# One of every 24 row gathers of a graph-attention kernel becomes a one-hot product on TensorE

## The chip, the cores and the metric

The kernel runs on one NeuronCore of one Trainium2 chip. The metric is the device time of one execution in microseconds (us). The core has five engines that run their own instruction streams and wait for one another through semaphores: TensorE (PE in the profile), VectorE (DVE), ScalarE (ACT), GpSimd (POOL) and SyncE (SP), which here issues most DMAs.

## The reference, cut to what matters

A graph of 6,250 nodes with 64 features and 206,250 edges, sorted by destination, goes through one mean-aggregating layer and three attention layers. Each attention layer is this (heads H = 2, 2, 1; C = 64 / H):

```python
q = (x @ Wq + bq).reshape(n, H, C)
k = (x @ Wk + bk).reshape(n, H, C)
v = (x @ Wv + bv).reshape(n, H, C)
e = (eattr @ We).reshape(-1, H, C)
kj = k[src] + e
alpha = jnp.sum(q[dst] * kj, axis=-1) / jnp.sqrt(C)
m = segment_max(alpha, dst); a = jnp.exp(alpha - m[dst])
a = a / (segment_sum(a, dst)[dst] + 1e-16)
vj = v[src] + e
out = segment_sum(a[..., None] * vj, dst)       # then + x @ Ws + bs
```

What the change is about is `k[src]` and `v[src]`: for each edge, 64 + 64 numbers of the row of its source node.

## The kernel before

The edges are cut into 202 blocks of 1,024. A block is T = 8 tiles of 128 edges, one edge per partition. Each attention layer first runs a node phase, which computes for all nodes a table `KV` of 128 float32 per node (k and v side by side) and a table `QT`, and stores both to DRAM. Then an edge pass goes over the blocks. For each block:

- POOL fetches the rows of the source nodes: `gathers` issues 8 indirect DMAs, one for each tile (L1621), into the tile buffer `G` (named `Gall` in the profile), of which there are three, one for each of three successive blocks. The row numbers come from `sdn`. The first gather of a block waits until PE has done step `aT` of the block three earlier.
- PE computes the edge part `e` (L896, L901: 512 columns, float32), picks the queries with a one-hot product (`q`, L921), transposes alpha (`aT`, L928), transposes the scan's result back (`Fb`, L933), carries maxima through one-hot products (`Mc` L936, `Mn` L948, `Me` L955) and sums the weighted values of a block (`fac` L966, `agg` L963).
- DVE adds and multiplies (`kj` L754, `vj` L759, `prod` L765, `alpha` L770), makes the one-hot tables (`OT` L733, `O` L722), does a running maximum (`scan` L784) and small work on the maxima (`fhi`, `fm`, `flo` L787 and L800, `cr` L807, `X` to `df` L811 to L825), weights the values (`vals` L842) and adds them to `acc` (L869, L890).
- ACT does the exponentials and some copies. SP issues the other loads.

The order of work is written by hand: `vector_step`, `tensor_step` and `scalar_step` each hold one step `t`, in which an engine works on five blocks at different stages (Z for block t+2, A for t+1, B for t, C for t-1, D for t-2). Three steps make one turn of the hardware loop, because the buffers have three slots. Each engine has one counting semaphore, and `after(e, engine, op, s)` waits until that engine has passed operation `op` of block `s`. A layer ends in a drain (`vector_drain`, `tensor_drain`) with its own order for the last blocks.

So in each step, PE's order is Fb, q, fac and agg, Mc, Mn, e, aT, Me, and the next step's Fb.

The mean layer's edge pass is simpler (PE: 512 columns `e`, `agg`, `q`), and has no gathers.

Of the kernel before, what the change touches and what calls it, by code (L numbers as in the profile page):

```python
# [16 lines left out]
T = 8  # L17
BE = 128 * T
BIAS = 6
W = 42  # L20
SL = 4


class Sizes:
    def __init__(self, n, e):
        self.n = n
        self.e = e
        self.blocks = -(-e // BE)
# [38 lines left out]
def build(nc, z, a, ctx):  # L67
    B, NCOL, NT, SM = z.blocks, z.nc, z.tiles, z.smax
    N = z.n

# [11 lines left out]
    WK = sb("WK", [128, NT, 64])  # L82
    hT = sb("hT", [65, NCOL])
# [14 lines left out]
    ioi = sb("ioi", [128, SM], I32)  # L98
    iof = sb("iof", [128, SM])
# [18 lines left out]
    rq = sb("rq", [128, SL, 4, 64])
# [4 lines left out]
    dnarrow = Gall[:, B * T:B * T + B * T // 2].bitcast(I16)  # L123
    sdn = [sb(f"sdn{u}", [128, 3 * T], I32) for u in range(3)]
# [39 lines left out]
    pIo = pM[:, 6 * T:6 * T + W]  # L164
    pFac = pG[0:66, 64:65]
    pFacS = pS[0:66, 200:201]

# [4 lines left out]
    D16 = dram("D16", [B, BE], I16)  # L172
    KV = [dram(f"KV{l}", [NCOL, 128]) for l in range(3)]
# [6 lines left out]
    def row(v, m):  # L180
# [7 lines left out]
    s_o = sem("out_landed")  # L188
    su_V, su_P, su_G, su_A = sem("setup_V"), sem("setup_P"), sem("setup_G"), sem("setup_A")
# [6 lines left out]
                 "cb", "cbh0", "cbh1", "rowf", "rowf4", "row1", "row2", "row12", "rowin", "thirds", "below", "third", "rowbase", "narrow", "iop"] + [f"qz{u}" for u in range(3)]  # L196
# [47 lines left out]
    def vector_setup(e):  # L244
# [92 lines left out]
        e.tensor_copy(pIo, iof[:, 0:W]).then_inc(su_V, 1)  # L337
        for u in range(3):
            e.memset(qw[u][:, :], 0.0).then_inc(su_V, 1)
# [20 lines left out]

    NG = -(-NT // 4)
# [7 lines left out]
    def node_phase(name, kind, w, H, kv, qt):  # L369
# [8 lines left out]
        before_kv, before_qt = {}, {}  # L378
        for c in range(NG if tables else 0):
            before_qt[c] = qt_landed[c % SL]  # L380
            qt_landed[c % SL] += 16
            if kv is not None:
                before_kv[c] = kv_landed[c % SL]
                kv_landed[c % SL] += 16
# [153 lines left out]
        def rows_A(e, c):  # L538
            g, m = c % SL, tiles_of[c]
            if before_kv[c]:  # L540
                e.wait_ge(s_kv[g], before_kv[c])
            e.wait_ge(own["P"], pP["mm", c])
            e.activation(stg[:, g, 0:m, 0:128], kv_bank[c % 2][:, 0:128 * m].rearrange("p (t c) -> p t c", t=m),
                         ACT.Copy).then_inc(own["A"], 1)

        def query_A(e, c):
            g, m = c % SL, tiles_of[c]
            both = q_bank[c % 2][:, 0:128 * m].rearrange("p (t c) -> p t c", t=m)
            if c >= SL:
                e.wait_ge(own["V"], pV["lo", c - SL])  # L550
            e.wait_ge(own["P"], pP["qs", c])
            e.activation(stg[:, g, 0:m, 128:192], both[:, :, 0:64], ACT.Copy).then_inc(own["A"], 1)
# [4 lines left out]
            e.activation(stq[:, g, 0:m, 0:64], stg[:, g, 0:m, 128:192], ACT.Copy).then_inc(own["A"], 1)  # L557

        def sync(e):
            if kv is not None:  # L560
                for c in range(NG):
                    e.wait_ge(own["A"], pA["ev", c])
                    e.dma_start(kv[512 * c:512 * c + 128 * tiles_of[c], :].rearrange("(t p) c -> p t c", p=128),
                                stg[:, c % SL, 0:tiles_of[c], 0:128]).then_inc(s_kv[c % SL], 16)
# [72 lines left out]
        def query_V(e, c):  # L637
            g, m4 = c % SL, tiles_of[c]
            hi, lo, mi = (stq[:, g, 0:m4, 64 * k:64 * k + 64] for k in range(3))
            rr = rq[:, g, 0:m4, :]  # L640
            e.wait_ge(own["A"], pA["hi", c])
            e.tensor_tensor(rr, stg[:, g, 0:m4, 128:192], hi, ALU.subtract).then_inc(own["V"], 1)
# [13 lines left out]
    def edge_pass(name, kind, l, heads, qtab, kvtab, eat):  # L656
# [9 lines left out]
        if att:  # L666
            order = {
                "V": ["A kj", "A vj", "B fhi", "B fm", "B flo", "B cr", "Z OT", "A prod", "A alpha", "C d1", "C d",
                      "Z cont", "Z last", "A flag", "A O", "B X", "B Mhi", "B Mm", "B Mlo", "B df", "C vals",
                      "D facc", "D acc", "A scan"],  # L670
                "P": ["B Fb", "A q", "D agg7", "B Mn", "Z e", "A aT", "B Me"],
                "A": ["A tb", "C w", "C wide", "A lb", "A Ob", "B fb", "B fbw"],
            }
        else:
            order = {
                "V": ["C acc", "Z O", "Z OT"],
                "P": ["A e", "B agg7", "A q"],
                "A": ["A relu"],
            }
# [13 lines left out]
        sums = [pG, pG, pG] if att else [pG, pQ, pY]  # L693
        columns = pIo if att else iof[:, 0:W]
# [16 lines left out]

        def ge16(e, sems, per, s):
            e.wait_ge(sems[s.slot], s.times(16 * per, 16 * per))


        def v_O(e, s):
# [3 lines left out]
            else:  # L720
                ge16(e, s_i, 1, s)
# [25 lines left out]

        def v_kj(e, s):
            u = s.slot
            ge16(e, s_g, T, s)  # L750
# [114 lines left out]
        def v_facc(e, s, fac=pFac, preset=False):  # L865
            if not preset:
                base_of[s.c] = base_at(e, s)
            c = acc[0:AR, bass.ds(base_of[s.c], 1)]
# [95 lines left out]

        def p_fac(e, s, fac=pFac):
# [39 lines left out]
        nV = place(["fhi1", "fm1", "flo1", "cr1", "d1_2", "d_2", "flag0", "vals2", "facc3", "acc3",  # L1005
# [7 lines left out]
        def vector_drain(e, n):  # L1013
# [4 lines left out]
            after(e, "V", "scan", s1)  # L1018
            e.wait_ge(dP, nP["Fb1"])
# [23 lines left out]
            ge16(e, s_g, T, s0)  # L1043
# [60 lines left out]
        def one_hot(e, s):  # L1104
# [4 lines left out]
                iof[:, 0:W].unsqueeze(1).to_broadcast([128, T, W]), ALU.subtract, ALU.is_equal)  # L1109
# [20 lines left out]
        def tensor_drain(e, n):  # L1130
# [7 lines left out]
            p_q(e, s0, T - 1).then_inc(dP, 1)  # L1138
            p_fac(e, s3)
            for j in range(T - 1):  # L1140
                p_agg(e, s3, j)
            p_agg(e, s3, T - 1).then_inc(dP, 1)
# [12 lines left out]
            for j in range(T - 1):  # L1155
                p_agg(e, s2, j)
            p_agg(e, s2, T - 1).then_inc(dP, 1)
# [10 lines left out]
            p_agg(e, s1, 0)  # L1168
# [5 lines left out]
            for j in range(1, 4):  # L1174
                p_agg(e, s1, j)
# [3 lines left out]
            for j in range(4, T - 1):  # L1179
                p_agg(e, s1, j)  # L1180
            p_agg(e, s1, T - 1).then_inc(dP, 1)
# [61 lines left out]

        def vector_step(e, t, on):
            pV = prog["V"]
            zt, at, bt, ct, dt = t + 2, t + 1, t, t - 1, t - 2
            if not att:
# [4 lines left out]
                if "Z" in on:  # L1252
                    v_O(e, zt).then_inc(pV, 1)
                    v_OT(e, zt).then_inc(pV, 1)
                else:
                    missing(e, "V", t, "O", "OT")
                return
            if "A" in on:
                v_kj(e, at).then_inc(pV, 1)
                v_vj(e, at).then_inc(pV, 1)  # L1260
            else:
                missing(e, "V", t, "kj", "vj")
# [31 lines left out]
            else:  # L1294
                missing(e, "V", t, "flag", "O")
            if "B" in on:
# [13 lines left out]
            if "D" in on:  # L1310
# [4 lines left out]
                v_facc(e, dt).then_inc(pV, 1)  # L1315
# [8 lines left out]
        def tensor_step(e, t, on):  # L1324
# [30 lines left out]
            if "D" in on:  # L1355
                after(e, "V", "acc", dt - 1)
                hold(e)
                p_fac(e, dt)
# [19 lines left out]
            else:  # L1378
                missing(e, "P", t, "aT", "aT")
            if "B" in on:  # L1380
# [152 lines left out]

        def load_rows(e, s, b, base):
# [33 lines left out]
        def sync_step(e, s):  # L1568
# [7 lines left out]
            load_rows(e, s, b, base)  # L1576

        def sync(e, ready):
# [3 lines left out]
            for c in range(3):  # L1582
                load_rows(e, At(0, c), *first_places[c])
            for c in range(3, 3 + z.peel):
                sync_step(e, At(0, c))
            with e.Fori(0, n) as i:
                for c in range(3 + z.peel, 6 + z.peel):
                    sync_step(e, At(i, c))

# [18 lines left out]
        def gathers(e, s):  # L1608
# [3 lines left out]
            for j in range(T):  # L1612
# [45 lines left out]
    def _(e):  # L1658
# [4 lines left out]
        for l in range(3):  # L1663
            att_pass[l]["E"](e, [(fold_V, l + 1), (s_dn, 16)])
            before[l]["S"](e)
            att_pass[l]["S"](e, before[l]["q_tables"])
# [30 lines left out]
    def _(e):  # L1697
# [6 lines left out]
        mean_end["V"](e, [(fold_V, 1)])  # L1704
        for l in range(3):
# [6 lines left out]
    def _(e):  # L1712
# [3 lines left out]
        mean_end["P"](e, [(fold_V, 1)])  # L1716
        for l in range(3):
            att_pass[l]["P"](e, [(Mb_V, l + 1), before[l]["done"]["A"], before[l]["done"]["V"]])
# [59 lines left out]
```

## Time and profile before

| | us |
|---|---|
| median of 3 runs | 6819.26 (6818.12 to 6822.41) |
| the profiled execution | 6818.34 |
| its span in the trace | 6816.5 |
| busy in the span: PE | 4422.8 (65%) |
| DVE | 4366.3 (64%) |
| ACT | 1118.9 (16%) |
| POOL | 4726.5 (69%) |

The span is what the trace covers; the profiled execution's own time is 1.8 us longer. The mean layer's edge pass runs from about 80 to 527 us, and the three attention passes with their node phases fill the rest. A busy share is an average over the engine; what an engine waits for, and for how long, has to be read from the waits.

### The profile page before, as it was taken

Reading aid. Unit: us, or ns where it says so; the run is one execution under the profiler, and the core shown is the slowest. Engines: PE = TensorE matmul, PEld = TensorE weight load, DVE = VectorE, ACT = ScalarE, POOL = GpSimd, SP = SyncE. Lnnn points to the kernel's source line nnn. Section 1 sums busy time; section 2 is a strip of 40 time slices with the busy share of each in tenths; the row PEclk is TensorE's granted clock in tenths of the full one; section 3 lists DMA queues with packets and bytes.
Section 4 is the critical chain, followed back from the end, with each engine's and each line's share of the span. In section 5 each row is a group of like instructions: output and inputs, shape, how many; then the busy total and the mean of one; then the engine's idle time right before and its main releaser. Section 6 shows DMA issues by size and latency. Waiting matters only on the chain. (4 is left out here: it accounts for less than half of the span.)

```text
span 6816.5 us, 149747 instructions
## 1 busy us (share of the span) xinstructions
PE 4422.8 (65%) x36620; PEld 3475.0 (51%) x36620; DVE 4366.3 (64%) x15732; ACT 1118.9 (16%) x4722; POOL 4726.5 (69%) x5116
## 2 busy tenths in 40 slices
PE   7996666666666667666666666667666666666665
PEld 5775444444444446444444444446444444444444
DVE  5556666666666666666666666666666666666666
ACT  3222111111111112111111111112111111111111
POOL 1224777777777775777777777775777777777776
PEclk9995555555555555555555555555555555555555
DMA  4553333333333333333333333333333333333333
GB/s 128 159 159 96 95 95 95 96 95 95 95 96 95 96 95 98 95 95 95 95 95 95 95 95 95 95 96 97 95 95 95 95 95 96 95 95 95 96 96 80
DMA packets 687682, 675.79 MB, mean 99 GB/s; under 512 B 369234, under 2 KB 506388, under 8 KB 687636
## 3 DMA queue, kind: packets, MB, share of 16 engines
q0 software_dynamic: 161600, 320.52, 18.3%
q1 hardware_dynamic: 496944, 301.76, 16.3%
q10 hardware_dynamic: 29092, 52.97, 2.6%
q8 instruction: 19, 0.31, 0.0%
q14 instruction: 27, 0.22, 0.0%
HBM read 652.96 MB, written 21.67 MB: 99 GB/s over the span
## 5 line engine op out<-in xcount | busy, mean ns | idle before, releaser
L1621 POOL DMA_INDIRECT Gall<-KV,sdn x4848 | 4590.0, 947 | 1517.0 <-issue 1380.9
L754 DVE TENSOR_TENSOR kj<-Gall,pE 128x512 f32<-128x512 f32 x603 | 414.4, 687 | 1973.4 <-DMA Gall<-KV,sdn 1971.3
L963 PE MATMUL pG<-O,vals 128*66 128x42 f32 (+1 forms) x10736 | 1291.9, 308 | 0.7 <-ACTq L1242 0.7
L963 PEld LDWEIGHTS pG<-O,vals 128*66 128x66 f32 (+1 forms) x10736 | 1200.8, 223 | 47.4 <-ACT vals L1002 28.4
L948 PE MATMUL pY<-fw,Ob 128*42 128x6 bf16 (+1 forms) x4800 | 255.1, 176 | 1139.9 <-DVE cr L807 1139.9
L994 ACT ACTIVATE vals<-dd 128x16 f32<-128x16 f32 (+1 forms) x606 | 131.6, 217 | 4679.5 <-DVE dd L834 4671.0
L948 PEld LDWEIGHTS pY<-fw,Ob 128*42 128x42 bf16 x4800 | 220.4, 121 | 1192.9 <-issue 1192.9
L896 PE MATMUL pE<-bd,ea 128*128 128x256 f32 x1212 | 739.9, 714 | 13.6 <-PEq L1242 13.6
L955 PEld LDWEIGHTS pM<-Mb,OTs 42*128 42x128 bf16 x4800 | 176.3, 101 | 921.1 <-issue 921.1
L901 PE MATMUL pE<-bd,ea 128*128 128x256 f32 x1212 | 642.8, 634 | 0.0
L955 PE MATMUL pM<-Mb,OTs 42*128 42x6 bf16 (+1 forms) x4800 | 209.9, 163 | 514.2 <-DVE df L825 511.8
L933 PE MATMUL pS<-ident,Fs 16*128 16x16 f32 (+1 forms) x600 | 150.0, 250 | 598.9 <-DVE Fs L784 567.9
L901 PEld LDWEIGHTS pE<-bd,ea 128*128 128x128 f32 x1212 | 408.7, 337 | 108.5
L933 PEld LDWEIGHTS pS<-ident,Fs 16*128 16x128 f32 (+1 forms) x600 | 105.9, 177 | 633.2 <-issue 633.2
L770 DVE TENSOR_REDUCE al<-kj 128x16 f32<-128x512 f32 (+1 forms) x603 | 414.3, 687 | 20.8
L733 DVE TENSOR_SCALAR OTs<-db,bfp 128x1024 bf16<-128x1024 int16 x808 | 408.0, 505 | 20.6 <-DMA dr<-in_dr 17.8
L759 DVE TENSOR_TENSOR vj<-Gall,pE 128x512 f32<-128x512 f32 x606 | 412.3, 680 | 0.0
L765 DVE TENSOR_TENSOR kj<-kj,pQ 128x512 f32<-128x512 f32 x603 | 408.4, 677 | 0.0
L842 DVE TENSOR_TENSOR vals<-vj,pE 128x512 f32<-128x512 f32 x597 | 401.4, 672 | 0.0
L1518 POOL DMA_DIRECT2D sdn<-in_sdn x202 | 108.8, 539 | 406.0 <-DVE OTs L733 334.5
L921 PE MATMUL pQ<-qw,OTs 128*128 128x64 bf16 x4848 | 367.5, 241 | 7.9 <-DVE OTs L733 5.2
L722 DVE SCALAR_TENSOR_TENSOR O<-sdn,bf,pM 128x336 f32<-128x336 int32 x603 | 329.1, 546 | 0.0
(223 smaller groups left out, 6539.9 us busy)
## 6 DMA issues: line engine op xcount, KB each, us to landing
db<-D SPq DMA_DIRECT2D x606, 256.0 KB
ea<-in_ea SPq DMA_DIRECT2D x606, 128.0 KB
Gall<-KV,sdn POOLq DMA_INDIRECT x4848
db<-D ACTq DMA_DIRECT2D x202, 256.0 KB, 3.5
qw<-QT SPq DMA_DIRECT2D x1818, 5.2 KB
dr<-in_dr SPq DMA_DIRECT2D x1212, 4.0 KB
ea<-in_ea SPq DMA_DIRECT2D x202, 64.0 KB, 3.3
sdn<-in_sdn SPq DMA_DIRECT2D x606, 12.0 KB
```

Source lines behind the costliest of these rows:

```text
L733: return e.tensor_scalar(OTs[u][:, :, :].rearrange("p j m -> p (j m)"), db[u][:, :], bfp[:, bass.ds(s.value(), 1)], None, ALU.is_equal)
L754: return e.tensor_tensor(kj[:, :, :], G[u][:, :, 0:64], pE[u][:, :].rearrange("p (j c) -> p j c", c=64), ALU.add)
L759: return e.tensor_tensor(vj[u][:, :, :], G[u][:, :, 64:128], pE[u][:, :].rearrange("p (j c) -> p j c", c=64), ALU.add)
L765: return e.tensor_tensor(kj[:, :, :], kj[:, :, :], pQ[:, :].rearrange("p (j c) -> p j c", c=64), ALU.mult)
L770: return e.tensor_reduce(al[u][:, 0:H * T].rearrange("p (h j) -> p j h", h=H), kj[:, :, :].rearrange("p j (h c) -> p j h c", h=H), AX.X, A ...
L842: return e.tensor_tensor(vals[u][:, :, 0:64].rearrange("p j (h c) -> p j h c", h=H), vj[u][:, :, :].rearrange("p j (h c) -> p j h c", h=H) ...
L896: return e.matmul(pE[u][:, 0:256], ea[u][:, 0:128], bd32[:, l, :], start=True, stop=True)
L901: return e.matmul(pE[u][:, 256:512], ea[u][:, 128:256], bd32[:, l, :], start=True, stop=True)
L948: return e.matmul(pmn[:, j, :], lhs, rhs, start=False, stop=j == T)
L955: return e.matmul(pme[:, j, :], OTs[u][0:W, j, :], Mb[:, 0:3 * H], start=True, stop=True)
L963: return e.matmul(out[0:AR, 0:W], vals[u][:, j, 0:AR], O[u][:, j, :], start=j == 0, stop=j == T - 1)
L1621: e.indirect_dma_start(G[u][:, j, :], None, kvtab, bass.IndirectOffsetOnAxis(ap=sdn[u][:, j:j + 1], axis=0)).then_inc(s_g[u], 16)
```

## The change

The table `KV` of a layer, 50 tiles of 128 nodes, is now also kept in SBUF (`KVS`). For every third block (`picks`), POOL issues 7 gathers and not 8. The eighth tile's rows come from TensorE: PE multiplies a one-hot table `oh` (128 nodes by 128 edges) with four tiles of `KVS` at a time (128x512, float32) and accumulates over all 50 tiles in the bank `pG`. That leaves, for each edge and each of four candidates (the node number's quarter), one row of 128 numbers, and DVE picks the right one with six small operations (`v_sel`) and writes it to the eighth tile of `G`. The 13 matmuls of such a pick are spread over three steps (4, 4 and 5, one of them with 256 columns), each share as `gp` between `aT` and `Me`. DVE makes the one-hot tables (`v_oh`, one in each step, behind `O`), from a row of keys `kb` that SP loads once in three steps from a small table `K16`. That table is made once, behind the mean layer, from source numbers which DVE collects in the mean pass (`v_src`).

Beside that: `agg` and `fac` write to the bank `pY` where they wrote to `pG`, `v_facc` waits for `aT` too, the node phase evicts k and v straight into `KVS` (no wait for a staging slot), and some small tables of the setup lie in `KVS` for the time of the setup.

```diff
+        def v_sel(e, s, inc, n):
+            u = s.slot
+            to = G[u][:, LAST, :]
+            e.tensor_scalar(quarter[:, :], sdn[u][:, LAST:T], 7, 3, ALU.logical_shift_right,
+                            ALU.bitwise_and).then_inc(sel_V, 1)
+            e.wait_ge(sel_V, sel_at(s, 0))
+            e.tensor_tensor(msk[:, :], ioq[:, :], quarter[:, :].to_broadcast([128, 4]),
+                            ALU.is_equal).then_inc(sel_V, 1)
+            e.wait_ge(sel_V, sel_at(s, 1))
+            after(e, "P", "gp", s - 1)
+            e.tensor_scalar(to, pPick[:, 0, :], msk[:, 0:1], None, ALU.mult).then_inc(sel_V, 1)
+            for k in range(1, 4):
+                e.wait_ge(sel_V, sel_at(s, k + 1))
+                i = e.scalar_tensor_tensor(to, pPick[:, k, :], msk[:, k:k + 1], to, ALU.mult, ALU.add)
...
+        def v_oh(e, s):
+            k = (s.slot - pick_slot) % 3
+            m, f = PIECE[k], FROM[k]
+            if k == 0:
+                e.wait_ge(s_k, s.times(16, 16 * (2 - first_pick // 3)))
+            return e.scalar_tensor_tensor(
+                oh[s.slot][:, 0:m, :], kb[:, :].unsqueeze(1).to_broadcast([128, m, 128]), prow[:, 0:1],
+                pQd[:, f:f + m].unsqueeze(2).to_broadcast([128, m, 128]), ALU.subtract, ALU.is_equal)
...
+        def p_gp(e, s):
+            k = (s.slot - pick_slot) % 3
+            after(e, "V", "oh", s)
+            hold(e)
+            if k == 0 and picks(s):
+                after(e, "V", "sel", s)
+                hold(e)
+            for n in range(PIECE[k]):
+                q = order_q[FROM[k] + n]
+                m = min(4, NT - 4 * q)
+                p = e.matmul(pG[:, 0:128 * m], oh[s.slot][:, n, :],
+                             KVS[:, 4 * q:4 * q + m, :].rearrange("p t c -> p (t c)"),
+                             start=k == 0 and n == 0, stop=k == 2 and n == PIECE[k] - 1)
+            return p
...
             if "A" in on:
-                v_kj(e, at).then_inc(pV, 1)
+                if picks(at):
+                    v_sel(e, at, pV, 1)
+                v_kj(e, at).then_inc(pV, 1 if picks(at) else 2)
                 v_vj(e, at).then_inc(pV, 1)
...
+            if made(zt):
+                v_oh(e, zt).then_inc(pV, 1)
...
+            if made(at):
+                p_gp(e, at).then_inc(pP, 1)
...
-            for j in range(T):
+            for j in range(T - 1 if picks(s) else T):
```

On TensorE, in the loop of the first attention pass, one step stood like this before (from `e` of block t+2 to the next step's `agg`; `ident,al` is `aT`, `Mb,OTs` is `Me`, `ident,Fs` is `Fb`):

```order
L896 MATMUL pE<-bd,ea 128x256
L901 MATMUL pE<-bd,ea 128x256
L702 REGISTER_ALU
L928 MATMUL pS<-ident,al 16x128
L702 REGISTER_ALU
L955 MATMUL pM<-Mb,OTs 128x6 x8
L702 REGISTER_ALU
L933 MATMUL pS<-ident,Fs 128x16
L921 MATMUL pQ<-qw,OTs 128x64 x8
L702 REGISTER_ALU
L966 MATMUL pG<-e,fb 66x1
L963 MATMUL pG<-O,vals 66x42 x8
```

After the change the same place reads:

```order
L1014 MATMUL pE<-bd,ea 128x256
L766 REGISTER_ALU
L1041 MATMUL pS<-ident,al 16x128
L766 REGISTER_ALU x2
L1088 MATMUL pG<-KVS,oh 128x512 x4
L766 REGISTER_ALU
L1068 MATMUL pM<-Mb,OTs 128x6 x8
L766 REGISTER_ALU
L1046 MATMUL pS<-ident,Fs 128x16
L1034 MATMUL pQ<-qw,OTs 128x64 x8
```

The share `gp` (L1088) now stands behind `aT` and ahead of `Me`, of the next step's `Fb` and of all that follows.

On VectorE, at the start of the loop's turn in which the block is a picked one, this stands ahead of `kj` (L866) and `vj` (L871):

```order
L834 TENSOR_SCALAR quarter<-sdn 128x1
L836 ISA
L837 TENSOR_TENSOR msk<-ioq,quarter 128x4
L839 REGISTER_ALU
L766 ISA
L841 TENSOR_SCALAR Gall<-pG,msk 128x128
L843 REGISTER_ALU
L844 SCALAR_TENSOR_TENSOR Gall<-pG,msk,Gall 128x128
```

Two more of the last row follow, then `kj`; `kj` was the first operation of the step before.

On GpSimd, the loop's body of the first attention pass (three blocks) was this before:

```order
L1630 ISA
L702 ISA
L1621 DMA Gall<-KV,sdn 128x128 x8
L702 REGISTER_ALU
L1621 DMA Gall<-KV,sdn 128x128 x8
L713 REGISTER_ALU
L702 REGISTER_ALU
L1621 DMA Gall<-KV,sdn 128x128 x8
```

And after the change:

```order
L1791 ISA
L766 ISA
L1782 DMA Gall<-KV,sdn 128x128 x8
L766 REGISTER_ALU
L1782 DMA Gall<-KV,sdn 128x128 x8
L791 REGISTER_ALU
L766 REGISTER_ALU
L1782 DMA Gall<-KV,sdn 128x128 x7
```

One gather of the three blocks' 24 is gone. Ahead of the loop 77 gathers stand where 80 stood; with 64 turns of the loop that makes 3 + 64 = 67 fewer in a layer, 201 in all.

## Rows read from the trace of the kernel before

**Rows 1.** The page: granted TensorE clock in 40 slices, and the group of gathers.

```profile
PEclk9995555555555555555555555555555555555555
...
L1621 POOL DMA_INDIRECT Gall<-KV,sdn x4848 | 4590.0, 947 | 1517.0 <-issue 1380.9
```

**Rows 2.** The waits between 3400 and 4400 us: us in total, times, longest.

```profile
DVE kj L754 <- DMA Gall<-KV,sdn: 328.1, 100, 4.1
POOL Gall L1621 <- issue: 229.8, 754, 0.3
...
PE pY L948 <- DVE cr L807: 185.2, 100, 2.7
```

**Rows 3.** The timeline of PE over one step: start, us, engine, line.

```profile
3500.21 1.22 PE L896 MATMUL pE<-bd,ea 128*128 128x256 f32 x2
...
3502.07 0.42 PE L928 MATMUL pS<-ident,al 128*16 128x128 f32 x1
3503.40 0.35 PE L955 MATMUL pM<-Mb,OTs 42*128 42x6 bf16 x8 [0.91 <-DVE df L825]
3504.75 0.26 PE L933 MATMUL pS<-ident,Fs 16*128 16x16 f32 x1 [1.00 <-DVE Fs L784]
3504.94 0.61 PE L921 MATMUL pQ<-qw,OTs 128*128 128x64 bf16 x8
...
3507.75 0.23 PE L936 MATMUL pY<-cb,onb 1*42 1x54 bf16 x1
3509.45 0.42 PE L948 MATMUL pY<-fw,Ob 128*42 128x6 bf16 x8 [1.46 <-DVE cr L807]
...
3509.84 1.22 PE L896 MATMUL pE<-bd,ea 128*128 128x256 f32 x2
```

**Rows 4.** Groups by form between 3400 and 4400 us: busy, mean ns.

```profile
L754 DVE TENSOR_TENSOR kj<-Gall,pE 128x512 f32<-128x512 f32 x100 | 68.8, 688 | 328.1 <-DMA Gall<-KV,sdn 328.1
...
L776 DVE TENSOR_TENSOR flg<-tb 16x127 f32<-16x127 f32 x100 | 28.4, 284 | 0.0
```

**Rows 5.** The timeline of PE in the mean layer's edge pass.

```profile
303.62 1.09 PE L963 MATMUL pY<-O,vals 128*65 128x42 f32 x16
304.53 0.41 PE L921 MATMUL pE<-qw,OTs 128*128 128x64 bf16 x8
304.77 1.10 PE L897 MATMUL pE<-bd,ea 128*128 128x512 f32 x2
305.72 0.50 PE L963 MATMUL pG<-O,vals 128*65 128x42 f32 x6
```

**Rows 6.** PE in stretches: length, busy (instructions), granted clock, DMA share, GB/s.

```profile
528.00:530.00 2.00, 0.82 (x14) 1.00 0.00 0
530.00:532.00 2.00, 1.06 (x10) 0.61 0.00 0
...
548.00:550.00 2.00, 2.00 (x11) 0.50 0.00 0
550.00:552.00 2.00, 2.00 (x16) 0.77 0.00 0
552.00:554.00 2.00, 0.75 (x7) 1.00 0.00 0
554.00:556.00 2.00, 0.00 (x0) 0.58 0.00 0
592.00:594.00 2.00, 2.00 (x11) 0.50 0.58 147
3400.00:4400.00 1000.00, 625.71 (x5000) 0.50 0.36 95
```

**Rows 7.** The timeline of PE where the dense stretch at 547 us begins.

```profile
547.17 1.06 PE L478 MATMUL pE<-ident,WK 128*64 128x128 f32 x4
```

**Rows 8.** The timeline of PE inside the stretch at 592 us.

```profile
592.83 1.92 PE L499 MATMUL pQ<-wn,hT 65*128 65x128 f32 x8
```

**Rows 9.** The timeline of POOL at the first attention layer's end.

```profile
2614.29 0.94 POOL L1621 DMA_INDIRECT Gall<-KV,sdn  x1 [0.31 <-issue]
```

**Rows 10.** The timeline of DVE there.

```profile
2613.25 0.40 DVE L784 TENSOR_TENSOR_SCAN Fs<-flg,pS 16x128 f32<-16x128 f32 x1
2615.37 0.17 DVE L787 TENSOR_TENSOR fw<-pS,lm 128x16 bf16<-128x16 f32 x1 [1.72 <-PE pQ L921]
...
2619.68 0.69 DVE L1044 TENSOR_TENSOR kj<-Gall,pE 128x512 f32<-128x512 f32 x1 [0.59 <-DMA Gall<-KV,sdn]
```

**Rows 11.** All engines in the same long stretch: PE, PEld, DVE, ACT, POOL busy, clock.

```profile
3400.00:4400.00 1000.00, 625.71 (x5000) 491.75 (x4998) 650.86 (x2396) 145.42 (x700) 756.49 (x800) 0.50 0.36 95
```

More of the change, by code:

```diff
@@ L21 @@
 SL = 4
+LAST = T - 1
 class Sizes:
@@ L123, in build @@
     dnarrow = Gall[:, B * T:B * T + B * T // 2].bitcast(I16)
+    srcT = sb("srcT", [128, 4 * KG])
+    kb = sb("kb", [128, 128], I16)
+    oh = [sb(f"oh{u}", [128, PIECE[2], 128]) for u in range(3)]
+    quarter = sb("quarter", [128, 1], I32)
+    msk = sb("msk", [128, 4])
+    prow = sb("prow", [128, 1])
+    ioW = sb("ioW", [128, W])
+    ioq = sb("ioq", [128, 4], I32)
     sdn = [sb(f"sdn{u}", [128, 3 * T], I32) for u in range(3)]
@@ L556, in query_A @@
             e.wait_ge(own["A"], pA["qf", c])
[L557 removed]
+            e.activation(stq[:, g, 0:m, 0:64], stg[:, g, 0:m, :], ACT.Copy).then_inc(own["A"], 1)
         def sync(e):
@@ L667, in edge_pass @@
             order = {
-                "V": ["A kj", "A vj", "B fhi", "B fm", "B flo", "B cr", "Z OT", "A prod", "A alpha", "C d1", "C d",
-                      "Z cont", "Z last", "A flag", "A O", "B X", "B Mhi", "B Mm", "B Mlo", "B df", "C vals",
+                "V": ["A sel", "A kj", "A vj", "B fhi", "B fm", "B flo", "B cr", "Z OT", "A prod", "A alpha", "C d1", "C d",
+                      "Z cont", "Z last", "A flag", "A O", "Z oh", "B X", "B Mhi", "B Mm", "B Mlo", "B df", "C vals",
                       "D facc", "D acc", "A scan"],
-                "P": ["B Fb", "A q", "D agg7", "B Mn", "Z e", "A aT", "B Me"],
+                "P": ["B Fb", "A q", "D agg7", "B Mn", "Z e", "A aT", "A gp", "B Me"],
                 "A": ["A tb", "C w", "C wide", "A lb", "A Ob", "B fb", "B fbw"],
@@ L710, in hold, with picks, rows_landed, v_src @@
             e.sem_inc(spare, 1)
+        def picks(s):
+            return s.slot == pick_slot and not (isinstance(s.i, int) and s.c < first_pick)
+        def rows_landed(e, s):
+            if s.slot == pick_slot:
+                full = first_pick // 3
+                n = s.times(16 * (T - 1), 16 * (T - 1 + full))
+                if isinstance(s.i, int) and s.c < first_pick:
+                    n = s.times(16 * T, 16 * T)
+                e.wait_ge(s_g[s.slot], n)
+            else:
+                ge16(e, s_g, T, s)
         def ge16(e, sems, per, s):
             e.wait_ge(sems[s.slot], s.times(16 * per, 16 * per))
+        def v_src(e, s):
+            ge16(e, s_i, 1, s)
+            return e.tensor_copy(srcT[:, bass.ds(s.value(), 1)], sdn[s.slot][:, LAST:T])
         def v_O(e, s):
@@ L1532, in load_db, with load_keys @@
             e.dma_start(db[u][:, :], D16[bass.ds(b, 1), :].to_broadcast([128, T * 128])).then_inc((s_l if att else s_d)[u], 16)
+        def load_keys(e, s):
+            if not (isinstance(s.i, int) and s.c == first_pick):
+                after(e, "V", "oh", s - 4)
+                hold(e)
+            e.dma_start(kb[:, :], K16[bass.ds(s.value(), 1), :].to_broadcast([128, 128])).then_inc(s_k, 16)
         def load_rows(e, s, b, base):
@@ L1576, in sync_step @@
             load_rows(e, s, b, base)
+            if att and picks(s + 2):
+                load_keys(e, s + 2)
         def sync(e, ready):
```

165 lines of the change are left out of this document (120 added, 45 removed).

## The prediction

> **What bounds the kernel now.** I read first the page's group of gathers: 4848 of them, 947 ns each [rows 1]. Then the waits in a long quiet stretch of the second attention pass, 3400 to 4400 us [rows 2]. DVE's `kj` waits for a gather's landing in each of the 100 steps, 3.3 us a step. POOL waits for nothing but its own issue, 0.3 us between two gathers. So one gather costs 0.947 + 0.30 = 1.247 us, eight make 9.98 us, and a step takes 10.0 us (100 steps in 1000 us). The edge passes run at POOL's pace. PE is busy 6.26 us of a step, DVE 6.51 us, ACT 1.45 us [rows 11]. PE's other waits (1.85 us a step for `cr`, and those for `df` and the scan [rows 2, 3]) follow from DVE starting late.
>
> The second thing to see is TensorE's clock. The page shows 9 to 10 tenths only in its first three slices, and 5 tenths from there on [rows 1]; in the stretch it is 0.50, the 1.2 GHz level [rows 6]. All PE durations of the attention passes are for that level. Since the change gives PE much work, the whole question is at which level it will run.
>
> **The gathers that go.** 67 in each of three layers, 201 in all. At 1.247 us each that is 250.6 us. They are worth this only while POOL stays the bound: three steps then take 23 x 1.247 = 28.7 us instead of 29.9, on average 9.56 us a step.
>
> **What PE gets.** The 13 products of a pick stream 6400 float32 columns over 128 rows. The nearest row at 1.2 GHz is `e`: 512 columns of the same form from 3500.21 to 3502.07, 1.86 us [rows 3]. 12.5 times that is 23.3 us in three steps, 7.75 us a step. At the full clock, `e` of the mean pass takes 305.72 - 304.77 = 0.95 us for 512 columns [rows 5], so 11.9 us in three steps, 3.97 us a step. These are the two ends.
>
> The rest of PE's step at 1.2 GHz, from start to start [rows 3]: `e` 1.86, `aT` 0.42, `Me` 0.35, `Fb` to `Mc` 3507.75 - 3504.75 = 3.00, `Mc` 0.23, `Mn` 3509.84 - 3509.45 = 0.39; sum 6.25. At 2.4 GHz `agg` takes 0.91 us (303.62 to 304.53) and `q` 0.24 [rows 5], against 1.96 or so and 0.54; with `e` 0.95 and the small ones left as they are, the rest is about 4.0 us. So a step holds **14.0 us of PE work at the low level, 7.95 us at the high one**, and POOL needs 9.56. At the low level PE would be the bound by far, at the high one not at all.
>
> **Which level.** The rows of the node phase tell what raises it. At 547.17 four groups of transposes of 128 rows begin, back to back [rows 7]; PE is busy 2.00 of 2.00 us, the clock 0.50 at first, and 0.77 in the slice 550 to 552, so it rose at 550.9, 3.7 us after the dense stretch began [rows 6]. It was still high when work stopped at 552.75, and fell at 554.3. After the mean pass, with PE only half busy from 527.3 on, it was 1.00 until 530 and 0.61 in the slice behind, so it fell at 530.4, 3 us after the dense work ended [rows 6]. Against that stands 592 to 594: PE busy 2.00 of 2.00 and the clock 0.50 [rows 6]; those matmuls have only 65 rows of 128 [rows 8]. `gp` has all 128 rows and follows `e` and `aT`, also of 128, with nothing between; the operands of L478 were one-hot too (the identity), and the clock rose. So I expect it to rise in each step that begins low.
>
> A step that begins low then goes so. The dense stretch `e`, `aT`, `gp` is 1.86 + 0.42 + 7.75 = 10.0 us at the low level. The first 3.7 us run low, the other 6.3 at about half price (1.86 to 0.95), 3.2 us: together 6.9. Behind it come `Me`, `Fb`, `q`, `fac`, `agg`, `Mc`, `Mn`: 3.97 us low, 2.6 us high. The sum is **9.5 to 10.9 us**. A step that begins high takes 7.95 us of PE. As the clock outlasts the dense work by 1.6 to 3 us by the rows, and the work behind it is 2.6 us, it should live through the gap in a part of the steps. With as many of one kind as of the other the mean is about (10.2 + 7.95) / 2 = 9.1 us, a little under POOL's 9.56. I take POOL as the bound, with a small margin. The trace speaks for a mean clock of 0.8 to 0.9 in the attention passes, against 0.50.
>
> The Trainium skill ("TensorE: Matmul & The Clock Gate", Part 1, on HAM oscillation and the psum-queue case) speaks against this: frequent short idles of PE between groups of matmuls let the clock swing between its two levels. By that rule alone each burst would begin low, at 9.5 to 10.9 us a step; it is the first rival below, and the trace bears it out as far as the clock fell at 530.4 and 554.3 after short pauses. The page also says that sustained busy time brings the high level; the stretch at 592 us does not bear that out.
>
> **What DVE gets.** `oh` in every step has 512 or 640 float32 columns. Nearest is `kj`, 512 columns, 0.688 us [rows 4]; by columns 0.69, 0.69 and 0.86, so 0.75 us a step. `sel` in every third: two tiny operations and four of 128 columns. The nearest row is `flg`, 127 columns, 0.284 us [rows 4]; six of these are 1.7 us as an upper end, four of them 1.1 as a lower, so 0.4 to 0.6 a step. DVE's 6.51 us become 7.8, under 9.56. But `sel` waits for the `gp` of the step before, and `kj`, `vj` and all that leads to `aT` stand behind it. From the end of `gp` on, DVE needs 1.7 for `sel`, some 1.3 for `kj` and `vj`, and about 2.4 to the end of `alpha`: 5.4 us. PE has `Me` to `e` meanwhile, 3.6 (high) to 5.8 us (low). So in one step of three PE waits up to 1.8 us at `aT`; on average 0.3 us a step. 9.1 becomes 9.4, still under 9.56.
>
> **The rest, small.** SP's load of `kb` is one more issue in three steps, of 32 KB, and a 64 KB gather goes; the key row is loaded over most of a step ahead of its use, and SP's queue has nothing behind it that is nearly late. `agg` in `pY` and the wait of `facc` for `aT` cost nothing: the DVE reaches `facc` behind `X` and `vals`, when `aT` is done. The mean pass gets one tiny DVE operation a step and stays bound by PE. Setup gets some eight tiny operations, 1 to 2 us. The node phases evict as much as before.
>
> Each layer's end gets longer. Before, the last gather was issued at 2614.29 [rows 9] and `kj` of the last block began at 2619.68, kept by its landing by only 0.59 us at the end; `fhi` stood at 2615.37, 1.72 us late behind `Fb` [rows 10]. Now `gp` and `sel` stand ahead of this `Fb` and `fhi`. The drain's chain starts some 3 to 4 us later. Three layers: 10 us.
>
> **The sum.** -250.6 + 10 (drains) + 2 (setup) + 3 (steps in which PE overruns) = -236. Against the profiled execution, 6818.3, that is 6583; it lies 0.9 us under the median of the runs, so I say **6583 us**, 3.5% faster. Its own range is 6560 to 6640.
>
> **The rivals.**
>
> *The clock swings, and PE becomes the bound (0.26).* If the clock falls behind every burst, or rises later than at 547, a step costs PE 9.9 to 10.9 us. For: the sum above has a margin of only 0.2 to 0.5 us; the clock fell twice after short pauses; a picked step's wait adds a pause. Against: a longer dense stretch than any in the attention passes so far. It decides at 9.97 us of PE a step, the present pace: above that the kernel is slower. At 10.2 to 10.8 us a step, 0.23 to 0.83 over 9.97, times about 600 steps: 6960 to 7320. A step of 10.2 is the likelier end.
>
> *The clock rises, but PE overruns in many steps (0.12).* The bound is PE at 9.65 to 9.95 us a step: 6630 to 6805.
>
> *The gain and the loss cancel (0.04).* PE's mean is near 9.97: within 0.2%.
>
> *The clock never rises (0.03).* As from 592 to 594. Then a step is 13.4 to 14.0 us: (3.4 to 4.0) x 600 = 2050 to 2400 more, 8900 to 9200.
>
> *The change is hidden (within 0.2%)*, because the gather is not the bound, has no row for it; POOL's only wait is its own issue.
>
> **How the numbers follow.** The forecast has 0.55, faster. With the overrun case faster has 0.67; same 0.04; slower 0.29. A change within 0.2% (14 us) can't be told from none here. The range goes from 6560, a little under the forecast with no cost but the drains, up to 6980, which takes in the overrun, the cancelling case and the nearer half of the swinging one: 0.54 + 0.12 + 0.04 + 0.11 = 0.81.
>
> **What would show it.** In the profile of the changed kernel: 4647 gathers at 1.247 us, with POOL waiting for nothing but issue; the granted clock at 0.8 to 0.9 in the attention passes; `gp` at 0.9 to 1.1 us for each 512 columns; three steps in 28.7 us; `kj` waiting for a gather less than 1 us a step; `sel` waiting for `gp`; a layer's drain 3 to 4 us longer. The prediction is wrong if POOL waits for `aT` before its first gather of a block, if `kj` no longer waits for a landing, or if the clock is under 0.7 on average: then PE is the bound.

## The result, and the profile after

The changed kernel takes 6616.46 us (median of 4 runs, 6608.92 to 6623.22), the kernel before 6818.86 us. The ratio is 0.9702, with a 95% interval of 0.969 to 0.9714: 3.0% faster. The forecast was 6583 us, 3.5% faster, so the sign and the mechanism hold, and about 33 us of the gain are missing. The profiled execution is the fastest of the four (6608.92 us, span 6607.3), 209 us under the one before; the rows below can account for what that execution lacks, about 26 us, and not for the 7.5 us between it and the median.

The page of the changed kernel, with the busy times, the clock in 40 slices, and the groups of gathers, of the new products and of `kj`:

```profile
PE 5853.9 (89%) x41850; PEld 3646.5 (55%) x41850; DVE 5189.8 (79%) x17757; ACT 1121.3 (17%) x4722; POOL 4546.2 (69%) x4915
...
PEclk9997888888888886888888888887888888888888
...
L1782 POOL DMA_INDIRECT Gall<-KV,sdn x4647 | 4409.7, 949 | 1473.2 <-issue 1371.3
L1088 PE MATMUL pG<-KVS,oh 128*128 128x512 f32 (+1 forms) x5226 | 2714.1, 671 | 13.2 <-DVE lm L819 4.9
...
L866 DVE TENSOR_TENSOR kj<-Gall,pE 128x512 f32<-128x512 f32 x603 | 409.0, 678 | 493.1 <-DMA Gall<-KV,sdn 469.4
```

There are 4647 gathers where there were 4848 [rows 1], each as long as before to 2 ns. The clock's digits are mostly 8, here and there 6 or 7, where they were 5. PE is busy 89% and DVE 79% of the span.

The waits between 3400 and 4400 us, which answer to [rows 2]:

```profile
POOL Gall L1782 <- issue: 234.4, 769, 0.3
...
PE pY L1061 <- DVE cr L919: 94.9, 61, 2.5
...
DVE kj L866 <- DMA Gall<-KV,sdn: 84.7, 49, 3.1
...
DVE Gall L841 <- PE pG L1088: 42.5, 31, 2.9
```

POOL still waits for hardly anything but its own issue. `kj` waits for a landing 84.7 us in 104 steps, 0.8 us a step, where it was 3.3, and in 49 of the steps only, where it was all: it is still the gathers that are late, but only just. The new wait is the selection's (L841) for the product, 42.5 us in 31 picks. PE still waits 0.9 us a step for `cr`, which is spare time.

PE over some three steps, the answer to [rows 3]. The first share of the product runs at the high clock, the second begins at the low one:

```profile
3502.79 3.67 PE L1088 MATMUL pG<-KVS,oh 128*128 128x512 f32 x8
3506.39 0.35 PE L1068 MATMUL pM<-Mb,OTs 42*128 42x6 bf16 x8
...
3508.46 0.20 PE L1049 MATMUL pY<-cb,onb 1*42 1x54 bf16 x1
3510.59 0.43 PE L1061 MATMUL pY<-fw,Ob 128*42 128x6 bf16 x8 [1.93 <-DVE cr L919]
...
3512.86 0.42 PE L1041 MATMUL pS<-ident,al 128*16 128x128 f32 x1
3513.07 4.48 PE L1088 MATMUL pG<-KVS,oh 128*128 128x512 f32 x10
...
3519.55 0.20 PE L1049 MATMUL pY<-cb,onb 1*42 1x54 bf16 x1
3521.16 0.42 PE L1061 MATMUL pY<-fw,Ob 128*42 128x6 bf16 x8 [1.41 <-DVE cr L919]
...
3531.35 0.36 PE L1061 MATMUL pY<-fw,Ob 128*42 128x6 bf16 x8
...
3538.61 0.34 PE L1061 MATMUL pY<-fw,Ob 128*42 128x6 bf16 x8
```

And PE in stretches over the same time, and over the long one (length, busy, granted clock, DMA share, GB/s):

```profile
3502.00:3504.00 2.00, 1.72 (x6) 1.00 0.18 43
...
3506.00:3508.00 2.00, 2.00 (x31) 1.00 0.90 216
3508.00:3510.00 2.00, 0.66 (x10) 1.00 0.26 48
3510.00:3512.00 2.00, 1.41 (x11) 0.64 0.29 75
3512.00:3514.00 2.00, 2.00 (x6) 0.51 0.18 47
3514.00:3516.00 2.00, 2.00 (x6) 1.00 0.47 103
...
3520.00:3522.00 2.00, 0.84 (x10) 0.70 0.27 66
3522.00:3524.00 2.00, 2.00 (x6) 0.50 0.18 49
3526.00:3528.00 2.00, 2.00 (x4) 0.59 0.86 184
3530.00:3538.00 8.00, 8.00 (x73) 1.00 0.45 108
3400.00:4400.00 1000.00, 897.43 (x6100) 0.86 0.39 98
```

Four products take 3506.39 - 3502.79 = 3.60 us, 0.90 us each, at the 2.4 GHz level. After the pause from 3508.7 to 3510.6 the clock is at the low level; it rises at 3514.0, 3.4 us after PE has begun dense work at 3510.59. This is the course that the prediction drew from 547 us. It is not the only one: after the next pause PE begins dense work at 3521.16, and the clock rises only at 3527.6, 6.5 us later. The step behind that (3531.35 to 3538.61) runs at the high level throughout. In the long stretch PE is busy 897.43 us in 104 steps, 8.6 us a step.

**Where 209 us come from.** I took the starts of all gathers from the trace and split the difference of the two profiled executions:

| | us |
|---|---|
| 201 gathers at the pace of before (1.2516 us from start to start, over 4842 of them) | -251.6 |
| from the start of the 24th gather of each layer to that of the 25th: 3.56, 5.41, 5.71 before; 7.70, 12.88, 12.07 now | +18.0 |
| the pace of all other gathers: 1.2538 in place of 1.2516 us | +10.5 |
| from a layer's last gather to the next layer's first: 55.4 and 54.4 before; 58.5 and 59.1 now | +7.9 |
| the end behind the last gather | +4.6 |
| the start ahead of the first gather | +1.4 |
| sum | -209.2 |

Three steps take 28.83 us (from the first gather of a block to that of the block three later, mean over the loops) where they took 30.03. The second and the third line were not in the prediction's sum at all. Most of the third is gathers that take over 1 us: they cost 9.2 us more than before (last section). The timeline of DVE at the head of the second attention layer shows what makes the second line:

```profile
2625.31 0.49 DVE L813 TENSOR_SCALAR OTs<-db,bfp 128x1024 bf16<-128x1024 int16 x1 [6.15 <-DMA dr<-in_dr]
...
2632.56 0.75 DVE L854 SCALAR_TENSOR_TENSOR oh<-kb,prow,pM 128x512 f32<-128x512 int16 x1 [6.31 <-DMA kb<-K]
2633.96 0.69 DVE L866 TENSOR_TENSOR kj<-Gall,pE 128x512 f32<-128x512 f32 x1 [0.65 <-DVEq L1373]
```

and that of SP why:

```profile
2626.90 1.40 SPq L1693 DMA_DIRECT2D qw<-QT  x3
2628.48 0.66 SPq L1700 DMA_DIRECT2D dr<-in_dr  x2
2629.19 0.37 SPq L1684 DMA_DIRECT2D kb<-K  x1
```

DVE's very first one-hot table waits 6.31 us for the key row, whose load stands on SP behind the 15 loads of the first three blocks' rows. `kj` and `vj` of block 0 stand behind it on DVE, and POOL may only refill the first buffer behind that `vj` (its wait then reads 11.94 us, put down to DVE `vj`).

### The profile page after: what moved, and what is told of

It reads as the page before. It is cut to its first block and busy times, and to the rows that moved or that the text cites. A ratio compares the mean times of both kernels' runs of the same rounds, so it can differ in the third digit from the quotient of the medians.

```text
span 6607.3 us, 168316 instructions
## 1 busy us (share of the span) xinstructions
PE 5853.9 (89%) x41850; PEld 3646.5 (55%) x41850; DVE 5189.8 (79%) x17757; ACT 1121.3 (17%) x4722; POOL 4546.2 (69%) x4915
## 5 line engine op out<-in xcount | busy, mean ns | idle before, releaser
L1782 POOL DMA_INDIRECT Gall<-KV,sdn x4647 | 4409.7, 949 | 1473.2 <-issue 1371.3
L1088 PE MATMUL pG<-KVS,oh 128*128 128x512 f32 (+1 forms) x5226 | 2714.1, 671 | 13.2 <-DVE lm L819 4.9
L1088 PEld LDWEIGHTS pG<-KVS,oh 128*128 128x128 f32 x5226 | 1137.3, 229 | 1285.4 <-issue 1256.4
L866 DVE TENSOR_TENSOR kj<-Gall,pE 128x512 f32<-128x512 f32 x603 | 409.0, 678 | 493.1 <-DMA Gall<-KV,sdn 469.4
L1076 PE MATMUL pY<-O,vals 128*66 128x42 f32 (+1 forms) x10576 | 755.6, 233 | 0.0
L1076 PEld LDWEIGHTS pY<-O,vals 128*66 128x66 f32 (+1 forms) x10576 | 683.6, 139 | 46.6 <-ACT vals L1130 33.3
L1009 PE MATMUL pE<-bd,ea 128*128 128x256 f32 x1212 | 537.8, 533 | 13.6 <-PEq L1373 13.6
L1061 PEld LDWEIGHTS pY<-fw,Ob 128*42 128x42 bf16 x4800 | 181.0, 104 | 573.0 <-issue 564.5
L854 DVE SCALAR_TENSOR_TENSOR oh<-kb,prow,pM 128x512 f32<-128x512 int16 (+1 forms) x606 | 472.0, 779 | 24.9 <-DMA kb<-K 23.4
L1014 PE MATMUL pE<-bd,ea 128*128 128x256 f32 x1212 | 485.4, 492 | 0.0
L871 DVE TENSOR_TENSOR vj<-Gall,pE 128x512 f32<-128x512 f32 x606 | 410.1, 677 | 0.0
L1014 PEld LDWEIGHTS pE<-bd,ea 128*128 128x128 f32 x1212 | 298.9, 247 | 60.3
L1109 ACT ACTIVATE Ob<-O 128x336 bf16<-128x336 f32 x606 | 282.9, 467 | 0.4
```

The costliest lines, as they stand in the source:

```text
L854: return e.scalar_tensor_tensor(oh[s.slot][:, 0:m, :], kb[:, :].unsqueeze(1).to_broadcast([128, m, 128]), prow[:, 0:1], pQd[:, f:f + m].un ...
L866: return e.tensor_tensor(kj[:, :, :], G[u][:, :, 0:64], pE[u][:, :].rearrange("p (j c) -> p j c", c=64), ALU.add)
L871: return e.tensor_tensor(vj[u][:, :, :], G[u][:, :, 64:128], pE[u][:, :].rearrange("p (j c) -> p j c", c=64), ALU.add)
L1009: return e.matmul(pE[u][:, 0:256], ea[u][:, 0:128], bd32[:, l, :], start=True, stop=True)
L1014: return e.matmul(pE[u][:, 256:512], ea[u][:, 128:256], bd32[:, l, :], start=True, stop=True)
L1061: return e.matmul(pmn[:, j, :], lhs, rhs, start=False, stop=j == T)
```

## The experiments

Each kernel is the changed one with the edit that is shown. e5 to e8 ran on a chip on which the kernel before took 9094.92 us and not 6818; nothing is concluded from their times (8831.25, 9636.66, 9492.73 and 9674.83 us). e9 to e12 are the same four kernels again, where the kernel before took 6818.70 and 6819.19 us. e3, e4, e10, e11 and e12 have one execution each.

**e1: the key row first.**

```diff
-            for c in range(3):
-                load_rows(e, At(0, c), *first_places[c])
             if att:
                 e.wait_ge(s_kn, 16)
                 load_keys(e, At(0, first_pick))
+            for c in range(3):
+                load_rows(e, At(0, c), *first_places[c])
```

> SP issues the load of the key row ahead of the 15 loads of the first blocks' rows, nothing else changes. Theory A (the shortfall sits at the layers' heads: DVE's first one-hot table waits 6.3 us for the key row, so the first vj comes late, and POOL's 25th gather with it): the waits at that gather (7.7, 12.9 and 12.1 us with the change) go back to about 3.6, 5.4 and 5.7 us, the time falls by 15 to 18 us to some 6600 us, ratio to the kernel before about 0.968. Theory B (the shortfall is PE overrunning in many steps): no change beyond 3 us, since the pace of the steps stays.

Measured: 6593.33 us (6590.59 to 6601.13, 5 runs), ratio 0.967 (0.9657 to 0.9684) to the kernel before. DVE at the same place, and POOL's 25th gather:

```profile
2620.18 0.48 DVE L813 TENSOR_SCALAR OTs<-db,bfp 128x1024 bf16<-128x1024 int16 x1 [6.68 <-DMA dr<-in_dr]
...
2621.28 0.75 DVE L854 SCALAR_TENSOR_TENSOR oh<-kb,prow,pM 128x512 f32<-128x512 int16 x1 [0.16 <-DVEq L1373]
```

```profile
2629.81 0.94 POOL L1782 DMA_INDIRECT Gall<-KV,sdn  x1 [6.29 <-DVE vj L871]
```

The wait for the key row is gone, and the starts around the 25th gather are 3.68, 7.24 and 7.28 us apart: 14.5 us of the 18 are back. In the first layer the distance is that of before, in the other two 1.8 and 1.6 us are left. The spans of the profiled executions differ by 15.2 us. Theory A holds at the heads, theory B does not: three steps still take 28.83 us. The medians differ by 23 us, 8 more than the profiles; the four runs of the change spread over 14 us, and whether the 8 us are more than that spread stays open. This is the fastest version here that leaves nothing out.

**e2 and e12: eight gathers, and all the new work.** The selection writes to a tile that nobody reads, and `kj` waits for eight landings in every block.

```diff
-            to = G[u][:, LAST, :]
+            to = dump[:, :]
...
-            for j in range(T - 1 if picks(s) else T):
+            for j in range(T):
```

> All the new work stays (one-hot tables, 13 products, selection), but POOL fetches all eight tiles of every block again, and the selection writes to a tile that nobody reads. Theory A (POOL's gathers are the bound, the new work is hidden in the steps): 8 x 1.25 = 10.0 us a step as before, plus what the change costs at heads and drains, 30 us: 6840 to 6870 us. Theory B (PE sets the pace at about 9.6 us and would be late by itself): also about 10.0 us a step; but then the granted clock and PE's waits differ little from the change's. The run gives the price of the new work without its gain; if it is over 6900, PE collides with the slower pace (the clock falls more often).

> The kernel of e2 again, for a profile: about 6855 us; 10.0 us a step at 1.25 us a gather, kj waiting 1 to 1.5 us a step for the landing, a mean clock of 0.8 to 0.86, and DVE's first one-hot table waiting 6 us for the key row in each layer, as with the change.

Measured: e2 6855.16 us (median of 5), ratio 1.0047 (1.0032 to 1.0063) from four of them; the fifth took 14311 us at a mean granted clock of 0.353 (last section). e12 6849.32 us. The waits of e12 between 3400 and 4400 us, and its clock:

```profile
POOL Gall L1776 <- issue: 235.9, 774, 0.3
...
DVE kj L860 <- DMA Gall<-KV,sdn: 113.7, 53, 3.5
```

```profile
3400.00:4400.00 1000.00, 876.01 (x5864) 0.85 0.37 96
```

Three steps take 30.06 us, against 30.03 before. So the new work is hidden in the steps, at 30 to 37 us for the whole kernel: in e12's profile 16.1 of 31.2 us stand again ahead of the 25th gathers (6.51, 12.53 and 11.77 us), and 7.9 in the pace of the others. The gathers alone are the gain.

**e3: the product over 64 of the 128 rows.** It leaves half of the nodes out, with the same columns, count and waits.

```diff
-                p = e.matmul(pG[:, 0:128 * m], oh[s.slot][:, n, :],
-                             KVS[:, 4 * q:4 * q + m, :].rearrange("p t c -> p (t c)"),
+                p = e.matmul(pG[:, 0:128 * m], oh[s.slot][0:64, n, :],
+                             KVS[0:64, 4 * q:4 * q + m, :].rearrange("p t c -> p (t c)"),
```

> The 13 products contract over 64 of the 128 rows of the table (half of the nodes are left out, so the fetched rows are wrong); columns, count, order and waits are the same. Theory A (what raises TensorE's clock is work over all 128 rows, as the stretch at 592 us of the kernel before suggests, and the gain hangs on the clock): the clock stays at 0.50 in the attention passes, a step is PE's dense sum, 13.4 us, the time about 6600 + 3.8 x 606 = 8900 us. Theory B (dense work of any kind raises it): 6600 us, mean clock 0.86 as with the change.

Measured: 8960.0 us, mean clock 0.529. PE between 3400 and 4400 us, and its group of products:

```profile
3400.00:4400.00 1000.00, 978.27 (x4221) 0.50 0.27 71
```

```profile
L1088 PE MATMUL pG<-KVS,oh 64*128 64x512 f32 x584 | 529.9, 1077 | 0.0
```

PE is busy 98% of the time, more than in any other run, and the clock is at the 1.2 GHz level in all three attention passes. Three steps take 40.3 to 40.5 us, 13.5 us a step. The expectation was 8900. So the change pays only because the clock rises, and in this kernel the same busy time with the product over 64 rows does not raise it: the difference of 2343 us between this run and the change is the price of the rival "the clock never rises". With the rows the run also leaves out half of the table's numbers; it can't part the two.

**e4 and e11: one and two more products in each step.** The first product of a share is done again, so that the sum is wrong.

```diff
-            for n in range(PIECE[k]):
+            todo = [0] * 1 + list(range(PIECE[k]))     # e11: [0] * 2
+            for x, n in enumerate(todo):
```

> Each step has one more product of 512 columns (the first of its share is done twice, so that the sum is wrong): 0.9 us more of PE at the high clock, 1.8 at the low one. Theory A (PE has spare time of 0.8 us or more a step, as its waits for cr show): still POOL's pace, 9.6 us a step, 6600 to 6650 us, the mean clock up to 0.90. Theory B (the margin is 0.2 us a step, as the prediction had it): 0.7 us a step more, about 7050 us.

> The kernel of e7 again, on a chip where the kernel before takes its usual time: two more products of 512 columns in each step than with the change. Theory A (PE's spare time at the high clock is between 0.8 and 1.6 us a step): PE becomes the bound, 9.8 to 10.3 us a step, 6720 to 7030 us, POOL waits for aT. Theory B (more PE work keeps the clock higher, and that pays for it): 6630 us at a mean clock of 0.95.

Measured: e4 6615.89 us, mean clock 0.908, three steps still 28.8 us. e11 7016.09 us, mean clock 0.926. PE in e4 and then in e11, between 3400 and 4400 us:

```profile
3400.00:4400.00 1000.00, 932.55 (x6318) 0.92 0.38 98
```

```profile
3400.00:4400.00 1000.00, 939.12 (x6126) 0.95 0.35 92
```

and what POOL and DVE wait for in e11:

```profile
DVE fw L899 <- PE pS L1046: 103.5, 54, 2.7
...
POOL Gall L1783 <- DMA sdn<-in_sdn: 71.8, 50, 2.0
DVE Gall L841 <- PE pG L1089: 67.1, 29, 2.4
```

One more product costs nothing; two make PE the bound: 30.75 us in three steps, 10.25 a step, and `kj`'s wait for a landing is no longer among the longest. Theory A holds in both, but the wait of POOL for `aT` that it named is not in the list: POOL's new wait is put down to the load of `sdn`. So PE's margin under POOL's 9.6 us lies between one product and two, 0.9 and 1.8 us a step. Two estimates fall near its lower end: 9.6 less the 8.6 us for which PE is busy is 1.0 us, and 10.25 less two products at 0.90 is 8.45 us, a margin of 1.1 us, which leaves aside that the clock was 0.95 in e11 and 0.86 in the change.

**e9: seven gathers, and none of the new work.** No one-hot tables, products, selection and key loads in the edge passes; the eighth tile of a picked block keeps old rows.

```diff
             if "A" in on:
-                if picks(at):
-                    v_sel(e, at, pV, 1)
-                v_kj(e, at).then_inc(pV, 1 if picks(at) else 2)
+                v_kj(e, at).then_inc(pV, 2)
...
-                p_aT(e, at).then_inc(pP, 1)
...
-            if made(at):
-                p_gp(e, at).then_inc(pP, 1)
+                p_aT(e, at).then_inc(pP, 2)
```

> POOL fetches seven tiles of each picked block, and all that should replace the eighth is left out (no one-hot tables in the edge pass, no products, no selection, no key loads; the eighth tile keeps old rows, so the output is wrong). Theory A (the gain is the gathers' issue time and nothing else, and the new work costs only at heads and drains and a little of POOL's pace): 201 x 1.2516 = 251.6 us less than before, 6565 to 6575 us, the clock at 0.54, kj waiting about 2.9 us a step. Theory B (part of the gain comes from TensorE's higher clock shortening chains): 6600 us or more here, since the clock stays low.

> The kernel of e5 again, on a chip where the kernel before takes its usual 6818 us (in e5's call it took 9095). Seven gathers for each picked block and none of the work that replaces the eighth. Theory A (the gain is the gathers' issue time and nothing else): 201 x 1.2516 = 251.6 us less than before, 6565 to 6575 us, the clock at 0.54, kj waiting about 2.9 us a step. Theory B (part of the change's gain comes from TensorE's higher clock): 6600 us or more here.

Measured: 6588.82 us (6584.89 to 6592.37, 4 runs), ratio 0.966 (0.9644 to 0.9676), clock 0.539. The waits between 3400 and 4400 us:

```profile
DVE kj L864 <- DMA Gall<-KV,sdn: 298.1, 104, 4.2
POOL Gall L1763 <- issue: 226.3, 742, 0.3
```

Theory A's range is missed by 14 us and theory B's is not reached: it is 230 us under the kernel before, not 251. The gathers follow one another at 1.2510 us even in the quietest places of a block, where it was 1.2485 in the runs of the kernel before, of the change and of e1; over 4641 gathers that is 11.6 us. Some 11 us more go into longer gathers (last section). Why the quiet spacing is longer is open. It goes with this kernel and not with the chip: a gather takes 0.947 us at the median in e9 and in e5, the same kernel on the other chip, and 0.944 in all others, e10 on e9's chip among them. Without the new work the kernel is 4.5 us faster than e1, and the two intervals overlap. That is a net figure: in the profiles e1 takes 13.3 us more than e9 at the start, the heads and the drains, and 11.5 us less in the pace of the gathers. So with the key row in its right place the new work costs between 4.5 and some 13 us, and whether the higher clock gives anything back this run can't tell.

**e10: the product behind `Me`.**

```diff
-            if made(at):
-                p_gp(e, at).then_inc(pP, 1)
-            else:
-                missing(e, "P", t, "gp", "gp")
             if "B" in on:
                 for j in range(T - 1):
...
             else:
                 missing(e, "P", t, "Me", "Me")
+            if made(at):
+                p_gp(e, at).then_inc(pP, 1)
+            else:
+                missing(e, "P", t, "gp", "gp")
```

> The share of the product stands behind Me and not ahead of it; nothing else changes. Me waits for DVE's Mlo. Theory A (PE needs its spare time, and gp is best started as soon as aT is done): PE now idles from aT until Mlo (1 to 2 us), and then runs gp in a stretch that is less dense ahead of it; Fb waits behind gp. A walk over the schedule with the rows' prices gives 10 to 12 us a step, 6850 to 8000 us. Theory B (there is spare time enough, the place is of no importance): 6600 to 6630 us.

> The kernel of e6 again, for the same reason: the share of the product stands behind Me and not ahead of it. Theory A (PE needs its spare time): it idles from aT until Mlo, Fb waits behind gp; 10 to 12 us a step, 6850 to 8000 us. Theory B (the place is of no importance): 6600 to 6630 us.

Measured: 8287.97 us. The timeline of PE, and its stretches inside this step and between 3400 and 4400 us:

```profile
3501.19 0.27 PE L1041 MATMUL pS<-ident,al 128*16 128x128 f32 x1
3503.21 0.35 PE L1068 MATMUL pM<-Mb,OTs 42*128 42x6 bf16 x8 [1.75 <-DVE df L937]
3503.49 7.14 PE L1088 MATMUL pG<-KVS,oh 128*128 128x512 f32 x10
3510.56 0.23 PE L1046 MATMUL pS<-ident,Fs 16*128 16x16 f32 x1
```

```profile
3502.00:3504.00 2.00, 0.79 (x9) 0.69 0.45 109
3504.00:3506.00 2.00, 2.00 (x3) 0.50 0.59 189
...
3400.00:4400.00 1000.00, 780.16 (x4684) 0.77 0.29 76
```

A step takes 12.1 to 12.5 us, over the range that was given (to 8000 us), in the direction of theory A. The place of `gp` ahead of `Me` is worth 1670 us: ahead of it, `gp` fills the time in which PE would wait for DVE's maxima. Behind it, PE waits 1.75 us first, the clock falls in the pause (it is at the low level from 3502.8 on; five products take 7.07 us here and 4.42 us in the change, 3513.07 to 3517.49), and `Fb`, for which DVE waits, comes later by both.

> Two more products of 512 columns in each step than with the change (the sum is wrong). One more cost nothing (6616 us, POOL's pace kept). Theory A (PE's spare time at the high clock is between 0.8 and 1.6 us a step): PE becomes the bound, 9.8 to 10.3 us a step, 6720 to 7030 us, POOL waits for aT. Theory B (more PE work keeps the clock higher, and that pays for it): 6630 us at a mean clock of 0.95.

> The kernel of the second experiment again, for a profile: about 6855 us; 10.0 us a step at 1.25 us a gather, kj waiting 1 to 1.5 us a step for the landing, a mean clock of 0.8 to 0.86, under the change's since PE has more idle time in a longer step.

These two are the expectations of e7 and e8, the kernels of e11 and e12 on the chip of the 9095 us.

## Why the prediction was right, and where it was short

- *POOL's pace is the bound, before and after.* Right. e9 removes the gathers alone and gives the gain (230 us), e12 adds the work alone and gives none (30 us more).
- *201 gathers at 1.247 us, 250.6 us.* The count is exact, the pace was assumed to stay. It grew from 1.2516 to 1.2538 us, 10.5 us that had no term.
- *The clock rises in each step that begins low, and lives through a part of the gaps; 0.8 to 0.9.* Right: 0.86. The rise came 3.4 us after dense work began in the one step shown and 6.5 us in the next, where the prediction had 3.7 for all. The record of the clock has 325 low stretches in the attention passes' 606 steps, so "as many of one kind as of the other" holds. e3 shows that without the rise the kernel would be slower by a third, 8960 us; the rival's price was 8900 to 9200.
- *PE at 9.4 us a step, under 9.56.* The size is wrong on the safe side: PE is busy 8.6 us a step. A step at the high level takes 7.26 us (3531.35 to 3538.61, four products), not 7.95; the two low ones shown take 9.2 us (3510.59 to 3519.75, five products) and 10.2 us (3521.16 to 3531.35, four), where the sum had 9.5 to 10.9. PE's wait at `aT`, put at 0.3 us a step, is 5.1 us in the 104 steps. e4 and e11 put the margin at 0.9 to 1.8 us and not at 0.2. The clock does swing, as the first rival said, but without making PE the bound; at 0.26 it was given too much.
- *`gp` at 0.9 to 1.1 us for 512 columns, `sel` 1.1 to 1.7 us, `oh` 0.75 us.* 0.90 and 0.78 us; `sel` takes 2.1 us where it need not wait (645.52 to 647.60 us), over the upper end: its four operations of 128 columns are 0.35 us each, not 0.28, and wait for one another.
- *The key row's load is hidden.* This is the step that failed, the largest of what is missing. In the loop it is (`oh` waits for `kb` 1.1 us in 1000). At a layer's head it is not: the prediction looked at what stands behind the load on SP, not at what stands ahead of it. 18 us, of which e1 wins 14.5 back.
- *Drains +10 us, setup +2, overruns +3.* Measured 12.4 us behind the last gathers (3.1, 4.7 and 4.6) and 1.4 us at the start; no overruns are seen in the steps, where POOL waits for PE 0.9 us in 1000.

The Trainium skill ("TensorE: Matmul & The Clock Gate", Part 1) was cited for the rule that short idles of PE let the clock swing. By that rule, the trace agrees that it swings (down at 3510.6, up at 3514.0); it disagrees where it would have every burst begin low, since the product at 3502.79 began high (1.00 in the stretch 3502 to 3504). Its other statement, that sustained busy time brings the high level, does not hold in e3: busy 98%, clock 0.50. There the measurement decides.

## What to carry to other kernels

Gathers that are bound by their issue on one engine could be replaced here by a much larger amount of work on another, because that work stands where this engine would idle (behind `Me` it cost 1670 us more), and because TensorE's clock rose under it: the same columns over half of the rows ran at 0.50 in place of 0.86 and cost 2343 us. Where a new operation is put into an in-order queue, look at the first turn of the loop too: there its operand's load may stand behind everything else, and whatever frees the first buffer waits with it. When a wait disappears from an engine, find out with one more unit of work how much is left: here one product more was free and two cost 400 us.

## What the runs showed of the hardware

- A gather takes 0.944 us at the median, but some take over 1.0 us: 120 of 4848 before, 164 of 4647 with the change and 194 in e9. Of the long ones, 67% before, 86% with the change and 82% in e9 overlap in time with DVE's `OT` operation (128x1024, int16 to bf16, 0.50 us), against 11 to 13% of the others. What they take over 0.944 us comes to 12.6, 21.8 and 23.7 us. That `OT` slows them is a correlation here; no run took it away.
- With the float32 products over 64 rows the clock stayed at the 1.2 GHz level for over 8000 us (e3, PE busy 98%); with those over 128 rows it rose in steps like the two shown, 3.4 and 6.5 us after dense work began, to a mean of 0.86.
- One of five executions of e2 ran 14311 us at a mean granted clock of 0.353. Its page shows the clock of the other executions for a quarter of the span, and then 1 to 2 tenths, under both of the levels seen elsewhere. No run of the kernel before did so.

```profile
PEclk9888888788411111111111111111111111122222
```

- On another chip the kernel before took 2276 us more, and e5 to e8 took 2242, 1349, 2477 and 2826 us more than the same kernels elsewhere. In e5 the gathers are as short as in e9 (949 and 952 ns on average), but POOL's idle time ahead of them is 3675.3 us and not 1453.9. The causes of both are open.
